# A two-layer sequence kernel: late row tiles planned in two parts, two token tiles normed beside the last rows, and a measured norm in its own tensors

## The chip, the cores and the metric

The kernel runs on one core of a Trainium2 chip. The metric is the device time of the whole program in microseconds (us). It has five kinds of engine queue: TensorE (PE), VectorE (DVE), ScalarE (ACT), GpSimd (POOL) and SyncE (SP), which issues most transfers. Each engine works through its own instructions in order, and engines wait for each other by semaphores only.

## What is computed

`x` is 4 sequences of 1024 tokens with 128 channels, 4096 tokens in all. Four steps follow one another, each on a layer norm of `x` and added to it:

```python
x = x + time_mixing(layernorm(x))   # linear recurrence per head, state = decay * state + k v
x = x + top1_ffn(layernorm(x))      # 8 experts, each token to the one with the largest logit:
                                    #   relu(x W1[e] + b1[e]) W2[e] + b2[e],  D_FF = 512
x = x + memory(layernorm(x))        # quaternion keys and values, cumulative sum along the sequence
                                    #   (this step also adds its own normed input)
x = x + top4_ffn(layernorm(x))      # 32 experts of width 64, 4 per token, and a shared one
```

All is float32. The first two are layer 1 (`mixing_and_top1`), the last two layer 2 (`memory_and_top4`).

## The kernel before

**Tiles.** The tokens are 8 token tiles of 512 (`TILES`, `TILE`), each 4 groups of 128 (`SUB`). `x_tok` stays on chip all the time. A stage of work on tile `i` is written as functions of a step number, 0 to 15; one engine's program is these functions called in a fixed order, each emitting this engine's part.

**Mixing.** `pipeline` (L345) runs, for each `i` and step, `scan(i)`, `tail(i-1)`, `send`, `pick(i-3)`, `ahead(i+1)`, `norm(i+2)`, `measure(i+3)` and `look(i-2)`. The layer norm of tiles 0 to 2 is made by `norm` on VectorE (statistics, steps 2 and 3) and GpSimd (L1331 to L1338, step 4: `var_eps`, `rstd`, `minus_mean`, `shift`). That of tiles 3 to 7 (`i >= MEASURED`) is made by `measure`: ScalarE sums and squares at step 1 (L1115 to L1122), takes the root at step 6 (L1128), and VectorE makes `rstd` and `shift` at steps 8 and 9 (L754, L757). Both use the same three tensors `minus_mean`, `rstd` and `shift`, so ScalarE's `measure(3)` waits for GpSimd's `shift` of tile 2 (`shift_ready, i`). ScalarE's `norm` (L1135) makes `xn` of them. `ahead` turns, mixes and projects: the `tanh` `m1` on ScalarE (L1149, L1157), mixes on TensorE (L481, L484), `lerp` on VectorE (L780), `xf` on GpSimd (L1350).

**Rows.** `pick` finds each token's expert and its place among that expert's rows; GpSimd scatters the normed rows by an indirect transfer into `rows_in` (one region per expert, L1376), each row with the number of the place in `results` that its outcome goes to (`token`). 39 row tiles of 128 rows (`ROW_TILES`) are then worked through: 12 (`EARLY_ROWS`) planned by `early_plan` when five token tiles are counted, and 27 planned by `late_plan` (L991) from the final counts. A plan is, per row tile, its expert and its first row. `late_plan` runs on VectorE inside `closing`, between `pick(7)` and `bias_out(3)`: about fourteen small operations, each behind the one before it by `all_put`, the larger on a grid of 27 row tiles by 8 experts.

For row tile `k` the engines do: SP fetches the rows (L403, three tiles ahead, when `result_row` of tile `k-1` is copied); TensorE transposes (L628), expands (L635, 8 matmul passes) and contracts (L644, 8 passes); ScalarE copies the expert's weights (L1242), the transposed rows (L1247) and makes `relu` (L1252); VectorE adds the first bias (`bias_hidden`, L973), copies the row numbers (L978) and adds the second bias (`bias_out`, L985); GpSimd sends the result rows by an indirect transfer into `results` (`give_back`, L1390). `late_rows` (L366) loops over the first 16 of the 27 (row tiles 12 to 27) and writes the last 11 (28 to 38) out one by one. Per row TensorE's order is `expand(k)`, transpose of `k+1`, `contract(k-1)`. VectorE has two `bias_part`s behind rows 28 and 29.

**Into layer 2.** SP waits until every row tile is stored, then fetches `results` for three token tiles (`bring_back`, L1739). `weave` (L1690) runs `norm(0)`, ten steps of `norm(1)`, `ahead(0)` with the rest of `norm(1)`, and then `body(i)` for each tile: per step `tail(i-1)`, `main(i)`, `ahead(i+1)`, `norm(i+2)`. In layer 2, `norm` is: step 3 VectorE adds the fetched results to `x_tok` (L1957), 4 statistics (L1962), 5 aggregates (L1969), 6 GpSimd makes `shift` (L2308 to L2315), 9 ScalarE makes `xn` (L2186), 12 TensorE transposes (L1797) and ScalarE copies (L2193). `ahead` is: 0 key projection (L1801, L1803), 1 ScalarE copies and squares, 2 VectorE reduces (L1976), 3, 5 and 7 ScalarE's key parts (L2207) and a root, 5 and 6 VectorE's maximum and reciprocal, 4 TensorE's value projection, 7 VectorE scales the values. `main` step 0 makes `bound`. VectorE meets `norm(2,3)` in `body(0)` at step 3.

The lines that the steps above name, beside the functions printed below:

```python
act.wait_ge(decay_ready, n + 1)                      # measure, ScalarE, step 1
act.wait_ge(shift_ready, i)
...
for i in range(BACK_RING):                           # SP, before weave
    bring_back(i)
```

Of the kernel before, what the change touches and what calls it, by code (L numbers as in the profile page):

```python
# [18 lines left out]
P = 128  # L19
BATCH, SEQ = 4, 1024  # L20
TOKENS = BATCH * SEQ
SUB = 4
# [33 lines left out]
def shape_constants():  # L56
# [8 lines left out]
    for k in range(P):  # L65
        for a in range(2):
# [25 lines left out]
LOOPED_ROWS = 16  # L92

B_PARTS = [("strict", P), ("ones", P), ("rank", EXPERTS), ("region", EXPERTS), ("first_row", EXPERTS),
           ("tile_no", ROW_TILES), ("tile_end", ROW_TILES), ("tile_start", ROW_TILES), ("token", GROUPS), ("empty", EMPTY_TILES),
# [4 lines left out]
def shape_constants_b():  # L100
# [13 lines left out]
    part["token"][:] = np.arange(TOKENS).reshape(P, GROUPS)  # L114
    part["empty"][:] = TOKENS + np.arange(EMPTY_TILES * P).reshape(P, EMPTY_TILES)
# [26 lines left out]
def mixing_and_top1(nc, block, x_tok, consts, state_space, rs_space, x_in, w_in, c_in, early, late, top1, b_in, w1_in, w2_in, b1_in, b2_in,  # L142
# [5 lines left out]
    with ExitStack() as ctx:  # L148
# [9 lines left out]
        weights = sb("weights", [P, A_WIDTH])  # L158
        spread = sb("spread", [P, HK * P], F32R)
# [6 lines left out]
        deviation = sb("deviation", [P, SUB])  # L166
        eps_gn = sb("eps_gn", [P, 1])
# [16 lines left out]
        xn = sb("xn", [P, SUB, P])  # L184
        xt = [sb(f"xt{h}", [P, TILE + 1]) for h in range(2)]
        dx = sb("dx", [P, TILE])
        mix1_dx = sb("mix1_dx", [P, P + E_MIX])
        heads_u = sb("heads_u", [P, P])
# [5 lines left out]
        decay = sb("decay", [P, 2, TILE])  # L194
        kk = sb("k", [P, 2, TILE])
        rr = sb("r", [P, 2, TILE])
        vv = sb("v", [P, TILE])
        v_hi = sb("v_hi", [P, 2, TILE], F32R)
        v_lo = sb("v_lo", [P, 2, TILE], F32R)
        table_call = sb("table_call", [P, 1])  # L200
        gate = sb("gate", [P, 2, TILE])
        rku = sb("rku", [P, TILE])
        bonus_v = sb("bonus_v", [P, 2, TILE])
        state = state_space[:, 0:HK * (SEQ + 1)].rearrange("p (j t) -> p j t", j=HK)
        rs = rs_space[:, 0:HK * TILE].rearrange("p (j t) -> p j t", j=HK)
        y_sum = sb("y_sum", [P, TILE])
        yc = sb("yc", [P, TILE])
        yc2 = sb("yc2", [P, TILE])
# [3 lines left out]
        z = sb("z", [P, TILE])  # L212
# [7 lines left out]
        b_ones = sb("b_ones", [P, EXPERTS])  # L220
# [17 lines left out]
        count = sb("count", [P, EXPERTS])  # L238
# [5 lines left out]
        top = sb("top", [P, EXPERTS + 1])  # L244
        climb = sb("climb", [P, EXPERTS])
        ended = sb("ended", [P, ROW_TILES, EXPERTS])
        climbed = sb("climbed", [P, ROW_TILES, EXPERTS])
# [18 lines left out]
        early_count = front[0][:, 4 * SUB * EXPERTS:(4 * SUB + 1) * EXPERTS]  # L266

# [46 lines left out]
        sums_ready, scaled_ready, square_ready, deviation_ready = (sem(name) for name in ("sums", "scaled_mean", "squares", "deviation"))  # L314
        stats_ready, moments_ready, var_ready = sem("stats_ready"), sem("moments_ready"), sem("var_ready")
# [25 lines left out]
        taken_over = [sums_ready, scaled_ready, square_ready, deviation_ready, scaled, spread_ready, mean_ready, stats_ready, moments_ready, var_ready, rstd_ready, shift_ready, xn_ready,  # L341
# [24 lines left out]
        def late_rows(engine, row, beside=None):  # L366
# [5 lines left out]
            for k in range(EARLY_ROWS + STORES * bodies, ROW_TILES):  # L372
                row(k, k % STORES, k // STORES)
                if beside:
                    beside(k - EARLY_ROWS - 8 * bodies)
# [7 lines left out]
        def _(sp):  # L383
# [51 lines left out]
            late_rows(sp, row)  # L435

        @block.tensor
        def _(pe):
# [115 lines left out]
            def pick(i, h, step):  # L554
# [19 lines left out]
                if step == 12:  # L574
# [4 lines left out]
                    if i == 0:  # L579
                        pe.wait_ge(route_set, 1)  # L580
                    if i == EARLY_TOKENS - 1:
# [145 lines left out]
            contract(ROW_TILES - 1, (ROW_TILES - 1) % 2)  # L727

        @block.vector
        def _(dve):  # L730
# [1780 lines left out]
```

## Time and profile before

| what | value |
|---|---|
| median of 3 runs | 820.4 us (819.52 to 821.27) |
| the profiled execution's own time | 819.28 us |
| its span, first to last instruction | 817.3 us |
| TensorE busy | 727.6 us, 89% |
| VectorE / ScalarE / GpSimd busy | 602.2 / 485.6 / 490.0 us |
| mean granted TensorE clock | 0.962 of full |

Times in the rows are microseconds from the start of the span. Busy shares are averages over stages with different limits; what counts for a stage is which wait in it ends last. In a timeline row, the brackets give how long the engine stood idle before the instruction and what released it; "issue" is time in which the profile shows nothing that it waited for. A granted clock of 0.50 is 1.2 GHz, 1.00 is 2.4 GHz. By time: mixing lasts to about 235, `closing` to about 285, the late rows to 342, the memory step to about 480, the top-4 step to the end.

### The profile page before, as it was taken

To read this page: it belongs to the slowest core of one execution; us is meant where nothing else is said; L and a number is where in the kernel's file an instruction comes from. 1 tells how busy PE (TensorE), PEld (TensorE's weight loads), DVE (VectorE), ACT (ScalarE), POOL (GpSimd) and SP (SyncE) were. 2 spreads that over 40 slices of the span, in tenths; PEclk is the share of its full clock that TensorE was granted. 3 is DMA by queue.
4 is the path that set the end of the run, shared out by engine and by line. 5 is a ranking of instruction groups with operands and counts; after the bars stand their busy time and mean duration, and the time that the engine had idled before them with its cause. 6 is when DMAs were issued, how large, how long until landed. Compare 5 with 4: busy or idle time off the path is not lost.

```text
span 817.3 us, 14378 instructions
## 1 busy us (share of the span) xinstructions
PE 727.6 (89%) x4027; PEld 549.6 (67%) x4028; DVE 602.2 (74%) x1377; ACT 485.6 (59%) x1045; POOL 490.0 (60%) x498
## 2 busy tenths in 40 slices
PE   4599999999868799668999979999999999999996
PEld 2345554555447689657888867777778787878784
DVE  3489999999965445347888758786868686868673
ACT  3567778664435367446566556666666665666553
POOL 3577668788753544436878745555555555555564
PEclk9889999999979999859999998999999999999999
DMA  8700000000011355210000036363636364646450
GB/s 246 244 0 1 0 1 14 8 8 14 14 40 44 107 137 142 67 41 28 14 1 1 2 74 137 74 149 79 145 83 140 84 140 89 134 93 132 100 122 13
DMA packets 38265, 60.47 MB, mean 74 GB/s; under 512 B 3776, under 2 KB 17728, under 8 KB 37808
## 3 DMA queue, kind: packets, MB, share of 16 engines
q1 hardware_dynamic: 35920, 54.93, 28.5%
q0 software_dynamic: 2272, 4.67, 1.7%
q8 instruction: 32, 0.52, 0.3%
q14 instruction: 41, 0.34, 0.1%
HBM read 51.31 MB, written 8.28 MB: 73 GB/s over the span
## 4 chain that ended last, share of the span: by engine, by line
PE 66%; DVE 17%; issue 7%; ACT 4%; POOL 2%; DMA 2%; DVEq 1%; another core or an unknown queue 0%; ACTq 0%; POOLq 0%; SPq 0%
DVE state_and_wide L803 4%; PE a_vb L635 4%; PE c_m L1861 4%; PE c_m L1826 4%; PE c_m L1863 3%; PE c_m L1862 3%; PE c_r L1842 3%; PE a_front L481 3%; PE a_vb L644 2%; PE a_y L644 2%; DVE a_vb L787 2%; PE c_v L1861 2%; PE c_r L1911 2%; PE c_r L1910 2%; PE c_r L1913 2%
## 5 line engine op out<-in xcount | busy, mean ns | idle before, releaser
L2379 POOL TENSOR_TENSOR d_hid_lo<-c_bound,d_hid_hi 128x512 fp32r<-128x512 f32 x136 | 175.6, 1292 | 141.3 <-ACT d_hid_hi L2289 139.9
L2289 ACT ACTIVATE d_hid_hi<-c_bound 128x512 fp32r<-128x512 f32 x136 | 85.1, 626 | 38.0 <-DVE c_bound L2160 36.8
L1367 POOL TENSOR_TENSOR ducts_and_memory_weights<-a_r,state_and_wide 128x512 f32<-128x512 f32 x64 | 75.0, 1181 | 25.2 <-DVE state_and_wide L803 19.8
L803 DVE TENSOR_TENSOR_SCAN state_and_wide<-a_decay,state_and_wide,a_vb 128x512 f32<-128x512 f32 x64 | 81.0, 1268 | 0.1
L2151 DVE TENSOR_TENSOR c_m<-c_bound,c_m 128x512 f32<-128x512 f32 x64 | 44.3, 691 | 23.5 <-PE c_m L1863 17.5
L2151 DVE TENSOR_TENSOR c_v<-c_bound,c_v 128x512 f32<-128x512 f32 x64 | 44.3, 692 | 22.0 <-PE c_v L1863 16.3
L1861 PE MATMUL c_m<-d_x_hi,d_hi 128*128 128x512 f32 x136 | 56.3, 414 | 3.6 <-DVE c_bound L2160 3.3
L2279 ACT ACTIVATE c_bound<-c_m 128x512 f32<-128x512 f32 x60 | 35.7, 595 | 33.7 <-PE c_m L1863 33.1
L2279 ACT ACTIVATE c_bound<-c_k 128x512 f32<-128x512 f32 x60 | 35.7, 595 | 33.4 <-PE c_k L1863 32.9
L1863 PE MATMUL c_m<-d_x_hi,d_lo 128*128 128x512 f32 x136 | 54.4, 400 | 0.0
L1862 PE MATMUL c_m<-d_x_lo,d_hi 128*128 128x512 f32 x136 | 54.0, 397 | 0.0
L787 DVE TENSOR_TENSOR a_vb<-a_k,a_vb 128x512 f32<-128x512 f32 x64 | 43.3, 688 | 8.1 <-PE a_vb L535 7.9
L973 DVE TENSOR_TENSOR a_lerp<-a_vb,b_b 128x512 f32<-128x512 f32 x39 | 27.0, 691 | 28.2 <-PE a_vb L635 20.0
L1350 POOL TENSOR_TENSOR a_xf<-a_lerp,a_xt 128x512 f32<-128x512 f32 x32 | 34.7, 1093 | 18.2 <-DVE a_lerp L780 18.1
L635 PE MATMUL a_vb<-a_td_hidden,a_m 128*128 128x128 f32 x312 | 42.5, 281 | 3.4 <-DVE a_lerp L973 1.8
L1376 POOL DMA_INDIRECT rows_in<-a_rows,a_index x32 | 31.9, 996 | 21.3 <-DVE a_index L953 15.2
L2160 DVE TENSOR_TENSOR c_bound<-c_v,state_and_wide 128x512 f32<-128x512 f32 x56 | 38.7, 691 | 7.0 <-DMA state_and_wide<-pair_weights 4.0
L481 PE MATMUL a_front<-a_m,a_weights 128*128 128x512 f32 x64 | 35.2, 644 | 8.5 <-ACT a_m L1149 8.4
L635 PEld LDWEIGHTS a_vb<-a_td_hidden,a_m 128*128 128x128 f32 x312 | 38.9, 197 | 4.4 <-issue 2.9
L2160 DVE TENSOR_TENSOR c_bound<-c_m,state_and_wide 128x512 f32<-128x512 f32 x56 | 38.7, 691 | 2.5 <-POOL d_hid_lo L2379 0.7
L534 PE MATMUL a_vb<-a_v_hi,a_spread 128*128 128x512 f32 x64 | 38.7, 605 | 0.6 <-issue 0.5
L1252 ACT ACTIVATE a_xf<-a_lerp 128x512 f32<-128x512 f32 x39 | 24.5, 629 | 22.8 <-DVE a_lerp L973 8.3
(376 smaller groups left out, 2151.1 us busy)
## 6 DMA issues: line engine op xcount, KB each, us to landing
state_and_wide<-pair_weights SPq DMA_DIRECT2D x64, 512.0 KB, 11.5
b_w<-in_w SPq DMA_DIRECT2D x2, 2048.0 KB, 12.1
state_and_wide<-in_moe SPq DMA_DIRECT2D x16, 204.0 KB
a_xf<-rows_in SPq DMA_DIRECT2D x39, 64.5 KB
state_and_wide<-results SPq DMA_DIRECT2D x8, 256.0 KB, 2.7
out<-c_read SPq DMA_DIRECT2D x8, 256.0 KB, 2.3
a_weights<-in_mixing SPq DMA_DIRECT2D x1, 1077.0 KB, 7.1
shape_consts<-in_consts SPq DMA_DIRECT2D x1, 744.0 KB, 4.4
```

The lines of the kernel that those rows point to most:

```text
L481: mm = pe.matmul(front[n % 3][:, :], w("mix2")[:, f * P:(f + 1) * P], m1[:, 0, :], start=True, stop=True)
L635: mm = pe.matmul(bank_h[h][:, f * P:(f + 1) * P], w1_now[:, h, f * P:(f + 1) * P], xin_t[:, h, :], start=True, stop=True)
L803: dve.tensor_tensor_scan(state[:, j, seq_cols(h, 1)], decay[:, h, :], vb[j % 3][:, :], first, ALU.mult, ALU.add).then_inc(scan_ready, 1)
L1367: pool.tensor_tensor(rs[:, j, :], rr[:, h, :], state[:, j, seq_cols(h, 0)], ALU.mult).then_inc(rs_ready, 1)
L1861: pe.matmul(out, weights_hi, moving_hi, start=start, stop=False)
L1862: pe.matmul(out, weights_hi, moving_lo, start=False, stop=False)
L1863: return pe.matmul(out, weights_lo, moving_hi, start=False, stop=stop)
L2151: dve.tensor_tensor(bank_3[r][:, :], silu[:, r, :], bank_3[r][:, :], ALU.mult).then_inc(product_ready, 1)
L2160: dve.tensor_tensor(hidden[:, r, :], bank_3[r][:, :], w_wide[:, u - 1, :], ALU.mult).then_inc(hidden_ready, 1)
L2279: act.activation(silu[:, r, :], bank_1[r][:, :], ACT.Silu).then_inc(silu_ready, 1)
L2289: act.activation(hid_hi[:, n % HALVES, :], hidden[:, r, :], ACT.Copy).then_inc(hi_ready, 1)
L2379: pool.tensor_tensor(hid_lo[:, n % HALVES, :], hidden[:, r, :], hid_hi[:, n % HALVES, :].bitcast(F32), ALU.subtract).then_inc(lo_ready, 1)
```

## The change

Three things are changed.

1. `measure` writes `minus_measured`, `rstd_measured` and `shift_measured` instead of the tensors that `norm` uses, with semaphores of their own (`inverse_ready`, `measured`). ScalarE's wait at step 1 is now for the previous measured tile, none for the first.
2. The late plan has two parts per expert, 16 parts in all (`PARTS`). The first part of an expert has as many whole row tiles as hold its rows of the first two token tiles (counted by a further matmul, `first_count`, in `pick(2)`); first parts come first. So the results of token tiles 0 and 1 (`FIRST_TOKENS`) are complete when 28 row tiles (`FIRST_ROWS`) are stored. `results` is laid out tile by tile, tiles 0 and 1 at its end; rows that a later row tile repeats go to a place aside (a minimum on VectorE in place of the copy of row numbers, in the last 11 row tiles).
3. The last 11 row tiles are emitted by `memory_and_top4` with a function `beside` called after each. SP fetches the results of tiles 0 and 1 behind row 30 and that of tile 2 when all rows are stored. The norms of tiles 0 and 1 and most of `ahead(0)` stand behind rows 30 to 38 by the table `BESIDE`; the value projection and the transposes of tile 1 follow the last row. Tensors that layer 2 lays its own over are allocated first (`mixing_operands`), and two PSUM banks change places. `weave` begins with `body(0)`.

The diff, cut to its core:

```diff
+FIRST_TOKENS = 2
+FIRST_ROWS = EARLY_ROWS + LOOPED_ROWS
+PARTS = 2 * EXPERTS
+def result_of(i):
+    return TILE * (i - FIRST_TOKENS) if i >= FIRST_TOKENS else OTHERS + ASIDE + TILE * i
...
+        def remaining(name, row, end):
+            def emit(beside):
+                for k in range(EARLY_ROWS + LOOPED_ROWS, ROW_TILES):
+                    row(k, k % STORES, k // STORES)
+                    beside(k - EARLY_ROWS - LOOPED_ROWS)
+                if end:
+                    end()
+            last_rows[name] = emit
...
 measure, VectorE
                 if step == 8:
                     dve.wait_ge(deviation_ready, i - MEASURED + 1)
-                    dve.wait_ge(xn_ready, i)
-                    dve.reciprocal(rstd[:, :], deviation[:, :]).then_inc(rstd_ready, 1)
+                    if i > MEASURED:
+                        dve.wait_ge(xn_ready, i)
+                    dve.reciprocal(rstd_measured[:, :], deviation[:, :]).then_inc(inverse_ready, 1)
...
 measure, ScalarE
                 if step == 1:
                     act.wait_ge(decay_ready, n + 1)
-                    act.wait_ge(shift_ready, i)
+                    need(act, measured, n)
...
 early_plan, VectorE
+                    put(dve.tensor_tensor(first_tiles[:, :], first_tiles[:, :], done[:, :], ALU.subtract))
+                    put(dve.tensor_scalar(part_tiles[:, 0:EXPERTS], first_tiles[:, :], 0.0, None, ALU.max))
+                    all_put()
+                    put(dve.tensor_tensor(first_upto[:, :], part_tiles[:, 0:EXPERTS], done[:, :], ALU.add))
+                    all_put()
+                    put(dve.scalar_tensor_tensor(first_upto[:, :], first_upto[:, :], float(P), route_const("first_row"), ALU.mult, ALU.add))
...
 late_plan, VectorE
-                grid = [P, LATE_ROWS, EXPERTS]
+                grid = [P, LATE_ROWS, PARTS]
...
+                put(dve.tensor_tensor(left[:, :], last_row, first_upto[:, :], ALU.subtract))
+                all_put()
+                put(dve.tensor_scalar(left[:, :], left[:, :], 0.0, float(P - 1), ALU.max, ALU.add))
+                put(dve.tensor_tensor(part_rows[:, first], last_row, first_upto[:, :], ALU.min))
+                put(dve.tensor_copy(part_rows[:, rest], last_row))
...
 layer 2
+        BESIDE = ((), (), ((0, 3), (0, 4)), ((0, 5), (0, 6), (1, 3), (1, 4)), ((0, 9), (1, 5)), ((0, 12), (1, 6)),
+                  (0, 1), (2, 3), (5,), (6, 7), ((1, 9),))      # a pair is norm(tile, step), a number ahead(0, step)
+        def start(norm, ahead, row):
+            for each in BESIDE[row]:
+                if isinstance(each, tuple):
+                    norm(each[0], each[0] % 2, each[1])
+                else:
+                    ahead(0, 0, each)
...
 weave
-            for step in range(STEPS):
-                norm(0, 0, step)
-            for step in range(NORMED_AT):
-                norm(1, 1, step)
-            for step in range(STEPS):
-                ahead(0, 0, step)
-                if step >= NORMED_AT:
-                    norm(1, 1, step)
...
 SP
-            for i in range(BACK_RING):
-                bring_back(i)
+            def beside(row):
+                if row == 2:
+                    sp.wait_ge(loaded["taken"], 1)
+                    stored_rows(FIRST_ROWS)
+                    for i in range(FIRST_TOKENS):
+                        bring_back(i)
+            last_rows["sp"](beside)
+            stored_rows(ROW_TILES)
+            bring_back(FIRST_TOKENS)
...
 TensorE, behind the rows
+            last_rows["pe"](beside)
+            ahead(0, 0, 4)
+            norm(1, 1, 12)
```

## Rows read from the trace of the kernel before

**Rows 1.** Busy time, share of the span and instructions (page, part 1).

```profile
PE 727.6 (89%) x4027; PEld 549.6 (67%) x4028; DVE 602.2 (74%) x1377; ACT 485.6 (59%) x1045; POOL 490.0 (60%) x498
```

**Rows 2.** Waits: who waited for whom: total, times, longest us.

```profile
ACT a_rate L1115 <- POOL a_shift L1338: 8.1, 1, 8.1
```

**Rows 3.** Windows: stretch, length, busy time per engine, PEclk, DMA share, GB/s.

```profile
316.00:324.00 8.00, 8.00 (x73) 7.92 (x72) 5.31 (x20) 6.03 (x13) 4.05 (x5) 1.00 0.47 126
```

**Rows 4.** Timeline of the last rows: start, us, engine, line, what, idle before.

```profile
321.17 0.96 POOL L1390 DMA_INDIRECT results<-a_xf,a_result_row  x1 [0.94 <-issue]
...
322.31 0.55 DVE L1102 TENSOR_TENSOR bias<-ducts_and_memory_weights,bias 1x384 fp32r<-1x384 f32 x1
322.89 0.69 DVE L973 TENSOR_TENSOR a_lerp<-a_vb,b_b 128x512 f32<-128x512 f32 x1
...
323.88 0.29 DVE L985 TENSOR_TENSOR a_dx<-a_y,b_b 128x128 f32<-128x128 f32 x1 [0.24 <-PE a_y L644]
324.78 0.69 DVE L973 TENSOR_TENSOR a_lerp<-a_vb,b_b 128x512 f32<-128x512 f32 x1 [0.60 <-PE a_vb L635]
...
329.30 0.63 ACT L1252 ACTIVATE a_xf<-a_lerp 128x512 f32<-128x512 f32 x1 [0.45 <-issue]
...
339.56 1.15 PE L644 MATMUL a_vb<-b_w,a_xf 128*128 x8 [0.74 <-DVE a_dx L985]
...
341.94 0.96 POOL L1390 DMA_INDIRECT results<-a_dx,a_result_row  x1 [0.93 <-DVE a_dx L985]
```

**Rows 5.** Timeline from the last row into layer 2.

```profile
344.32 1.30 SPq L1739 DMA_DIRECT2D state_and_wide<-results  x3
...
347.43 0.69 DVE L1957 TENSOR_TENSOR x_tok<-x_tok,state_and_wide 128x512 f32<-128x512 f32 x1 [6.28 <-DMA state_and_wide<-results]
348.16 0.87 DVE L1962 BATCH_NORM_STATS2 c_stats<-x_tok 128x6 f32<-128x128 f32 x4
...
350.26 1.05 POOL L2311 TENSOR_TENSOR c_rstd<-c_var_eps,ducts_and_memory_weights 128x4 f32<-128x4 f32 x1
...
351.96 1.65 ACT L2186 ACTIVATE c_xn<-x_tok,c_shift,c_rstd 128x128 f32<-128x128 f32 x4 [12.54 <-POOL c_shift L2315]
...
353.75 1.09 PE L1797 MATMUL c_x<-ident,c_xn 128*128 128x128 f32 x4 [13.04 <-ACT c_xn L2186]
...
360.41 1.22 ACT L2207 ACTIVATE c_key<-c_k 128x256 f32<-128x256 f32 x4
...
367.13 0.68 DVE L1957 TENSOR_TENSOR x_tok<-x_tok,state_and_wide 128x512 f32<-128x512 f32 x1
...
377.82 1.16 PE L1803 MATMUL c_k<-ducts_and_memory_weights,c_xt 128*128 128x128 f32 x8
```

**Rows 6.** Timeline of the first mixing stage, 36 to 52 us.

```profile
36.64 0.31 ACT L1115 ACTIVATE a_rate<-x_tok 128x128 f32<-128x128 f32 x1 [8.09 <-POOL a_shift L1338]
...
39.74 0.57 ACT L1149 ACTIVATE a_m<-a_front 128x512 f32<-128x512 f32 x1
...
42.48 0.75 DVE L780 SCALAR_TENSOR_TENSOR a_lerp<-a_front,a_weights,a_dx 128x512 f32<-128x512 f32 x1 [6.85 <-PE a_front L481]
...
43.31 1.09 POOL L1350 TENSOR_TENSOR a_xf<-a_lerp,a_xt 128x512 f32<-128x512 f32 x1 [5.72 <-DVE a_lerp L780]
...
50.85 1.09 POOL L1350 TENSOR_TENSOR a_xf<-a_lerp,a_xt 128x512 f32<-128x512 f32 x1 [0.42 <-DVE a_lerp L780]
```

**Rows 7.** Timeline of VectorE, late plan and what follows it.

```profile
266.28 0.38 DVE L1005 TENSOR_TENSOR a_ended<-a_end_tile,b_consts 128x216 f32<-128x216 f32 x1
...
268.57 0.28 DVE L985 TENSOR_TENSOR a_xf<-a_y,b_b 128x128 f32<-128x128 f32 x1
```

**Rows 8.** Windows of TensorE: stretch, length, busy time, PEclk, DMA share, GB/s.

```profile
274.00:276.00 2.00, 0.24 (x2) 1.00 0.14 33
...
343.00:344.00 1.00, 0.00 (x0) 0.50 0.20 66
```

**Rows 9.** Chain that ended last: start, us, what.

```profile
245.02 2.73 PE a_vb L635 x16
```

More of the change, by code:

```diff
@@ L364, in pick_step, with late_rows @@
             return step + 4 if i == EARLY_TOKENS - 1 else step
-        def late_rows(engine, row, beside=None):
+        def late_rows(engine, row):
             bodies = LOOPED_ROWS // 8
@@ L371, in late_rows @@
                     row(STORES * b + EARLY_ROWS + n, (EARLY_ROWS + n) % STORES, b + (EARLY_ROWS + n) // STORES)
[L372 to L375, printed above, removed]
+        last_rows = {}
+        def remaining(name, row, end):
[6 more added lines that the diff above has]
+            last_rows[name] = emit
         MEASURED = 3
@@ L580, in pick @@
                         pe.wait_ge(route_set, 1)
+                    if i == FIRST_TOKENS:
+                        pe.matmul(first_count, ones_b[:, :], total[:, h, :], start=True, stop=True)
                     if i == EARLY_TOKENS - 1:
@@ L1131, in norm @@
                 if step == (8 if i < MEASURED else 1):
-                    act.wait_ge(shift_ready, i + 1)
+                    if i < MEASURED:
+                        act.wait_ge(shift_ready, i + 1)
+                        by, less = rstd, shift
+                    else:
+                        act.wait_ge(measured, i - MEASURED + 1)
+                        by, less = rstd_measured, shift_measured
                     need(act, xt_ready, i)
@@ L1135, in norm @@
                         a = act.activation(xn[:, s, :], x_tok[:, SUB * i + s, :], ACT.Identity,
-                                           bias=shift[:, s:s + 1], scale=rstd[:, s:s + 1])
+                                           bias=less[:, s:s + 1], scale=by[:, s:s + 1])
                     a.then_inc(xn_ready, 1)
@@ L1431, in _ @@
             late_rows(pool, row)
-            give_back(ROW_TILES - 1, (ROW_TILES - 1) % STORES)
+            remaining("pool", row, lambda: give_back(ROW_TILES - 1, (ROW_TILES - 1) % STORES))
         for each in taken_over:
             nc.release_semaphore(each)
+        return last_rows
 QUATS, QC = P // 4, 4
@@ L1946, in end, with beside @@
                     mm.then_inc(yt_out, 1)
-            pe.wait_ge(bias_ready, 1)
-            pe.wait_ge(loaded["taken"], 1)
+            def beside(row):
+                if row == 5:
+                    pe.wait_ge(bias_ready, 1)
+                    pe.wait_ge(loaded["taken"], 1)
+                start(norm, ahead, row)
+            last_rows["pe"](beside)
+            ahead(0, 0, 4)
+            norm(1, 1, 12)
             weave(pe, norm, ahead, main, tail, look, route, unit, end)
@@ L2174, in end, with beside @@
                                       bank_z[:, :].rearrange("p (s c) -> p s c", s=SUB), ALU.add).then_inc(out_ready, 1)
-            dve.wait_ge(loaded["taken"], 1)
+            def beside(row):
+                if row == 2:
+                    dve.wait_ge(loaded["taken"], 1)
+                for each in BESIDE[row]:
+                    if isinstance(each, tuple):
+                        norm(each[0], each[0] % 2, each[1])
+                    elif each < 7:
+                        ahead(0, 0, each)
+            last_rows["dve"](beside)
+            ahead(0, 0, 7)
             weave(dve, norm, ahead, main, tail, look, route, unit, end)
@@ L2297, in end, with beside @@
                     act.activation(y_sb[:, :], bank_y[h][:, :], ACT.Copy).then_inc(y_ready, 1)
+            def beside(row):
+                if row == 2:
+                    act.wait_ge(loaded["taken"], 1)
+                start(norm, ahead, row)
+            last_rows["act"](beside)
+            norm(1, 1, 12)
             act.wait_ge(moe_loaded, 16 * PIECES)
-            act.wait_ge(loaded["taken"], 1)
             weave(act, norm, ahead, main, tail, look, route, unit, end)
@@ L2383, in end, with beside @@
                 pass
-            pool.wait_ge(bias_ready, 1)
-            pool.wait_ge(loaded["taken"], 1)
+            def beside(row):
+                if row == 3:
+                    pool.wait_ge(bias_ready, 1)
+                    pool.wait_ge(loaded["taken"], 1)
+                start(norm, ahead, row)
+            last_rows["pool"](beside)
             weave(pool, norm, ahead, main, tail, look, route, unit, end)
```

201 lines of the change are left out of this document (133 added, 68 removed).

## The prediction

> **What bounds the kernel now.** I read the busy shares first: TensorE is busy 89% of the span, VectorE 74% [rows 1], so a change pays only where TensorE stands idle. The table of waits then names such places, and two belong to this change. One is early: ScalarE waits 8.1 us at L1115 for GpSimd's `shift`, and `m1`, for which TensorE waits, stands behind it on ScalarE [rows 2]. The other is between the layers. In the late rows TensorE has no gap (8.00 of 8 us at full clock from 316 to 324 [rows 3]), and they go by at one per 1.9 us (bias additions at 322.89 and 324.78 [rows 4]). But the last row tile's contraction starts at 339.56, its result is sent at 341.94, the fetch of the results goes out at 344.32, the addition that needs it starts at 347.43, and TensorE waits 13.04 us until the transposes of tile 0 [rows 5]; they start right behind the four `xn` of 351.96.
>
> **Part 1, the measured norm in own tensors.** Before, `measure(3)` writes `minus_mean`, so ScalarE must wait until GpSimd has made `shift` of tile 2. Its idle time of 8.09 us ends at 36.64, so it was free at 28.55; its eight passes and what belongs to them last until `m1` at 39.74, 3.1 us [rows 6]. With own tensors the wait goes: `m1` starts at 28.55 + 0.05 + 3.1 = 31.7, 8.0 us earlier. What is late next? VectorE: it waits 6.85 us for the mix (42.48), so it is free at 35.63 [rows 6]. By then the first mix is there (`m1` 31.7, its tanh 0.57, a matmul of under 2 us even at half clock). The first `lerp` moves 42.48 - 35.63 = 6.85 us forward, and later ones by up to ScalarE's 8.1. GpSimd is the tighter one: `shift` of tile 2, which frees ScalarE at 36.6, and one state product of the size of an `xf`, 1.1 us, keep it until about 37.6, while before it began its first `xf` at 43.31: 5.7 us forward. From there to the end of the fifth (50.85 + 1.09 = 51.94) took 8.6 us though five `xf` and one product of 1.09 to 1.27 are 6.7; with VectorE ahead of it they go back to back: about 44.4, 7.5 us forward [rows 6]. Behind it stand `v_lo` and the next stage's spreading, so I take **7.5 us**; the ends are 5.7 (only the first `xf`'s gain lasts) and 8.1 (the whole wait). ScalarE still meets the wait for tile 2's `shift` in `norm(2)`, at 36.5, but the `tanh` behind it isn't due before 40.
>
> **Part 2, the plan in two parts.** `late_plan` gets 16 columns for 8. Its 27 x 8 comparison takes 0.38 us [rows 7]; at twice the elements each of the four such passes costs about 0.22 us more (the row less some 0.15 us for a pass with few elements), 0.9 us, and one more dependent step 0.2 us. It ends right where the waiting `bias_out(3)` starts (268.57 [rows 7]), and TensorE waits for that: +1.1 us. The three operations in `pick(2)` and four in `early_plan`, some 0.2 us each with their waits, stand on a VectorE that is nearly full there: 1.4 us at most, half counted. Sum **+1.8 us**, ends 0 and 3. The extra count matmul and the `min` for the cast cost nothing that shows. A contiguous fetch instead of a strided one I cost at nothing: each partition still reads 2 KB.
>
> **Part 3, two tiles normed beside the last 11 rows.** First what it can give. The order on VectorE has `norm(2,3)` in `body(0)`, which needs tile 2's results and so every row. It ran at 367.13; the same addition for tile 0 started 3.1 us behind the fetch [rows 5]. If the rows ended as before, it could now run at 344.32 + 3.1 = 347.4, so the transition gains 19.7 us less S, where S is by how much the inserted work delays the last row.
>
> Now S. A row leaves VectorE 0.6 us between a `bias_out` and the next bias addition (323.88 + 0.29 to 324.78), and an inserted bias rounding of 0.55 us fitted into such a gap (322.31) [rows 4]. ScalarE has about 0.4 us a row (0.45 before 329.30 [rows 4]), TensorE nothing. All queues are in order. I carried each engine's order through rows 30 to 38 with these durations:
> - Row 30. Row 27's results are sent at 321.17; by the last row (341.94 to 344.32) they are stored 2.4 us later, so the fetch goes out at 323.6 and lands at 326.6. VectorE has been free since 324.17: it stands 2.5 us, then 0.68 for the addition and 0.87 for the statistics. Row 31's bias addition stands behind this wait, and `relu`, contraction and GpSimd's return behind that. Less the gap of 0.6 and slips: 3.2 us.
> - Rows 31 and 32. GpSimd begins the norm only behind `give_back(30)` (0.8 until it starts, 0.96); then 0.2, 1.05 (the power, 350.26), 0.2 and 0.2 with their waits. VectorE's statistics of tile 1 wait for the first of these, ScalarE for the last, and then ScalarE has 1.65 us of `xn` [rows 5] ahead of row 32's `relu`: 4.3 us.
> - Row 33: transposes 0.45 on TensorE, copy 0.6 on ScalarE behind them, and `relu` behind that: 2.1 with what is left of the row before. Row 34: the key projection takes TensorE 1.5 (its eight passes 1.16 [rows 5]; the bias pass and a gap 0.4), then ScalarE two copies of 0.5 to 0.6: with the slack of the late row 0.9 beyond. Row 35: 0.6 of key parts (four took 1.22) and the root, which waits for VectorE's reduction (0.69, as for any 128x512): 1.3. Rows 36 to 38: two more pairs of key parts, a reciprocal of under 1, `xn` 1.65, partly in slack: 1.2.
>
> S = 3.2 + 4.3 + 2.1 + 0.9 + 1.3 + 1.2 = **13.0 us**. No row of before shows such a mix, so the ends: S can't be below the 1.9 us added to TensorE, which has no gap; were nothing hidden and five rows at half clock, S = 8.2 (VectorE) + 7.4 (ScalarE) + 2 (GpSimd) + 2.9 + 6 (TensorE) = 26.5. The transition then gains 19.7 - 13.0 = 6.7 by the fetch. VectorE's own way there is slightly longer: contraction issued to 340.45 + 13.0 = 353.45, then value projection 1.5, values 1.1, first `bound` 0.64, sums 0.9, next key projection 1.5, square 1.1, reduction 0.7, each with a hand-over of 0.05 to 0.3: 361.1 against 367.13. I take **6.0 us**.
>
> **The clock, and a rule against the change.** In the trace TensorE's granted clock stayed at full through a stretch in which it worked 0.24 of 2 us (274 to 276), and was at half in the third microsecond after the last contraction [rows 8]. The new waits of rows 31 and 32, some 3 to 4 us each, lie between the two. The Trainium skill, "TensorE: Matmul & The Clock Gate", section "HAM oscillation — how this bites in real kernels", says that a loop whose matmuls wait for transfers each time falls back to the slow clock and pays its return each time. Counted by rows: eight row matmuls take 0.9 us at full (two times eight and a transpose in the pitch of 1.9) and 1.4 at half clock (245.02: 16 in 2.73 [rows 9]), so five rows with both at half clock cost up to 5 us on TensorE, of which 2 to 3 come through behind the other waits.
>
> **The sum.** -7.5 + 1.8 - 6.0 = -11.7 us. The profiled execution took 819.28 (span 817.3 and 2.0 around it), so 807.6; the median of the runs is 1.1 above it: **808.7 us**.
>
> **The rivals.**
> - The rows hide the norms better (S about 6, as VectorE's waits overlap ScalarE's): 808.7 - 7 = 801.7. For it: the bias rounding that cost nothing. Against: the wait for the fetch on VectorE has nothing beside it.
> - The transition gives nothing (S about 19, the clock at half through five rows and the row loads late behind 512 KB of fetches): 808.7 + 6 = 814.7. For it the gaps named above.
> - Part 1's gain is given back in stage 1, since GpSimd has the products of stage 0 still to do: 3 of 7.5 left, 813.
> - Slower than before: the eleven last rows become a chain of four engines. VectorE waits for the fetch, GpSimd for VectorE behind its own sends, ScalarE for GpSimd, TensorE for ScalarE, in every row with work beside. It decides once S passes 19.7 + 7.5 - 1.8 = 25.4; at the upper end of 26.5, 821.5, and a little beyond with body(0) at half clock, 823. Against it: only rows 30 to 32 hold a fetch or GpSimd's chain.
>
> **How the numbers follow.** Forecast 0.55 (own range 804.5 to 813), better hidden 0.14, nothing from the transition 0.15, given back 0.05, slower 0.07; 0.04 for sums that cancel. A difference of 0.2% is about what a measurement can tell from none. Faster 0.88, same 0.04, slower 0.08. The range leaves out the best tenth of the hidden case and the slow ones: 801 to 817.
>
> **What would show it.** ScalarE's wait at L1115 gone from the start, `m1` at about 31.7, `closing` some 6 us earlier, a late plan of 4.8 us for 3.7. In the last rows: VectorE waiting 2 to 3 us for `come_back` behind row 30, the contraction of row 31 over 3 us late, 11 rows in some 34 us rather than 21, and `norm(2,3)` near 355 instead of 367.13. The forecast is wrong if the row pitch stays near 2 us (then 800), or if clock and pitch fall for all 11 rows.

## The result and the profile after

| | before | after |
|---|---|---|
| median of 4 runs each | 820.12 us (819.52 to 821.27) | 808.56 us (806.41 to 809.93) |
| profiled execution, its span | 819.28, 817.3 us | 809.93, 808.1 us |
| mean granted clock | 0.962 | 0.972 |

The ratio is 0.9852, with a 95% interval of 0.9828 to 0.9877. 808.7 us was predicted. The profiled execution was the slowest of the four after, so the two traces differ by only 9.2 us of span. All ratios are of fast executions; a single slow one, of 1839.72 us in e11, stays out.

I compare the traces by *lead*: how much earlier an instruction starts in a changed kernel's trace than the same one in the trace before. The lead is 7.5 us from stage 1 on (first spreading of `v` at 48.05 for 55.55), 6.7 behind `pick(2)`, 5.7 at 247, 3.3 at row 28's bias addition (315.88 for 319.19), -9.8 at the last contraction, 10.2 at `norm(2,3)`, 11.0 through the memory step and 9.2 at the end.

Mixing, timeline of ScalarE, GpSimd and TensorE after. ScalarE's wait of [rows 2] is gone, `m1` starts at 31.87 for 39.74, the five `xf` end at 44.4, and the wait for tile 2's `shift` is met at `xn` instead:

```profile
31.87 0.57 ACT L1253 ACTIVATE a_m<-a_front 128x512 f32<-128x512 f32 x1
36.92 1.65 ACT L1239 ACTIVATE a_xn<-x_tok,a_shift,a_rstd 128x128 f32<-128x128 f32 x4 [2.68 <-POOL a_shift L1442]
42.26 2.15 POOL L1454 TENSOR_TENSOR a_xf<-a_lerp,a_xt 128x512 f32<-128x512 f32 x2
48.05 0.47 PE L599 MATMUL a_vb<-a_v_hi,a_spread 128*128 128x512 f32 x1 [0.72 <-issue]
```

The late plan, timelines of VectorE. Before, from its first operation to `bias_out(3)` (268.57 [rows 7]), 3.6 us:

```profile
264.98 0.15 DVE L997 TENSOR_TENSOR a_count<-a_tail,b_consts 128x8 f32<-128x8 f32 x1
```

After, its first operation, the first of the four wide passes and `bias_out(3)`, 5.1 us from first to last:

```profile
260.04 0.15 DVE L1083 TENSOR_TENSOR a_left<-a_tail,a_first_upto 128x8 f32<-128x8 f32 x1
261.59 0.61 DVE L1097 TENSOR_TENSOR a_decay<-a_part_end,b_consts 128x432 f32<-128x432 f32 x1
265.11 0.28 DVE L1071 TENSOR_TENSOR a_xf<-a_y,b_b 128x128 f32<-128x128 f32 x1
```

The last rows, timelines after, which answer to [rows 4, 5]. VectorE waits for the fetch, GpSimd for VectorE, ScalarE for GpSimd's `shift`, and TensorE for ScalarE; the last contraction is at 349.37 for 339.56, the third tile's addition at 356.91 for 367.13:

```profile
323.39 0.69 DVE L2081 TENSOR_TENSOR x_tok<-x_tok,state_and_wide 128x512 f32<-128x512 f32 x1 [2.52 <-DMA state_and_wide<-results]
325.66 0.63 ACT L1356 ACTIVATE a_xf<-a_lerp 128x512 f32<-128x512 f32 x1 [3.84 <-DVE a_lerp L1055]
326.43 2.07 PE L711 MATMUL a_y<-b_w,a_xf 128*128 x8 [3.11 <-ACT a_xf L1356]
326.82 0.96 POOL L1495 DMA_INDIRECT results<-a_dx,a_result_row  x1 [4.21 <-DVE c_moments L2093]
329.71 1.65 ACT L2320 ACTIVATE c_xn<-x_tok,c_shift,c_rstd 128x128 f32<-128x128 f32 x4 [2.34 <-POOL c_shift L2455]
332.02 1.41 PE L711 MATMUL a_vb<-b_w,a_xf 128*128 x8 [2.04 <-ACT a_xf L1356]
338.70 0.60 ACT L2335 ACTIVATE c_key<-c_k 128x512 f32<-128x512 f32 x1 [2.19 <-PE c_k L1920]
349.37 1.15 PE L711 MATMUL a_vb<-b_w,a_xf 128*128 x8 [0.90 <-ACT a_xf L1356]
356.91 0.69 DVE L2081 TENSOR_TENSOR x_tok<-x_tok,state_and_wide 128x512 f32<-128x512 f32 x1 [0.26 <-DMA state_and_wide<-results]
```

Windows after (the column behind the five engines' busy times is the granted clock). The first three lie in the rows, the fourth where TensorE meets the top-4 step:

```profile
326.00:328.00 2.00, 1.57 (x7) 1.57 (x8) 0.89 (x6) 1.09 (x3) 1.15 (x2) 0.50 0.13 37
328.00:330.00 2.00, 1.97 (x12) 1.73 (x10) 1.44 (x5) 0.29 (x1) 1.46 (x4) 0.66 0.11 37
334.00:336.00 2.00, 2.00 (x12) 2.00 (x11) 0.00 (x0) 1.63 (x3) 1.24 (x3) 0.50 0.07 20
486.00:488.00 2.00, 2.00 (x6) 1.53 (x5) 0.28 (x4) 0.83 (x2) 0.20 (x1) 0.50 1.06 222
```

Over the whole span the clock was at half for 62 us before and 45 after; TensorE was busy in 37 of these before, 33 after.

### The profile page after: what moved, and what is told of

Its sections match the earlier page's. It is cut to its first block, busy times and chain, and to the rows that moved or that the text cites. A ratio compares the mean times of both kernels' runs of the same rounds, so it can differ in the third digit from the quotient of the medians.

```text
span 808.1 us, 14393 instructions
## 1 busy us (share of the span) xinstructions
PE 728.6 (90%) x4028; PEld 550.1 (68%) x4029; DVE 605.7 (75%) x1387; ACT 484.4 (60%) x1045; POOL 490.4 (61%) x498
## 4 chain that ended last, share of the span: by engine, by line
PE 44%; DVE 6%; issue 1%; ACT 1%; DMA 1%; POOLq 0%; DVEq 0%; SPq 0%; POOL 0%; ACTq 0%
PE c_m L1978 3%; PE c_r L1959 3%; PE c_m L1980 3%; PE c_m L1979 3%; PE c_m L1943 3%; PE c_v L1978 2%; PE c_v L1980 2%; PE c_k L1978 2%; PE c_r L2028 2%; PE c_v L1979 2%; PE c_r L2027 2%; PE c_r L2030 2%; PE c_k L1979 2%; PE c_k L1980 2%; PE c_o L2030 2%; PE c_o L2028 2%
## 5 line engine op out<-in xcount | busy, mean ns | idle before, releaser
L702 PE MATMUL a_vb<-a_td_hidden,a_m 128*128 128x128 f32 x312 | 44.4, 289 | 3.4 <-DVE a_lerp L1055 2.1
L702 PEld LDWEIGHTS a_vb<-a_td_hidden,a_m 128*128 128x128 f32 x312 | 40.9, 205 | 4.4 <-issue 2.9
L1454 POOL TENSOR_TENSOR a_xf<-a_lerp,a_xt 128x512 f32<-128x512 f32 x32 | 34.7, 1095 | 10.5 <-DVE a_lerp L848 10.4
L1495 POOL DMA_INDIRECT results<-a_xf,a_result_row x20 | 19.2, 961 | 28.7 <-DVE a_xf L1071 15.5
## 6 DMA issues: line engine op xcount, KB each, us to landing
state_and_wide<-pair_weights SPq DMA_DIRECT2D x64, 512.0 KB, 11.5
```

Source lines behind the costliest of these rows:

```text
L702: mm = pe.matmul(bank_h[h][:, f * P:(f + 1) * P], w1_now[:, h, f * P:(f + 1) * P], xin_t[:, h, :], start=True, stop=True)
```

## The experiments

Each ran five times or more, in turns with the kernel before on the same chip. Ratios are to that one; in us they are times 820.

**e1 and e2: parts alone.** e1 is the kernel before with the measured tensors only:

```diff
-                    dve.wait_ge(xn_ready, i)
-                    dve.reciprocal(rstd[:, :], deviation[:, :]).then_inc(rstd_ready, 1)
+                    if i > MEASURED:
+                        dve.wait_ge(xn_ready, i)
+                    dve.reciprocal(rstd_measured[:, :], deviation[:, :]).then_inc(inverse_ready, 1)
 (and shift_measured, minus_measured likewise)
```

> The kernel before with nothing but the measured norm in tensors of its own. Theory (the wait at the first measure is worth 7.5 us and the gain lasts to the end, since every later stage is bound by its own engines): 7.5 us faster than before, about 812.5. Rival (part of the lead is swallowed by the closing and the rows, where it fell from 7.5 to 3.3 us in the changed kernel, and not by the planning): 3 to 4 us faster, about 816.5.

Measured: 814.55 us (before 821.13), ratio 0.9917 (0.9893 to 0.9941): -6.8 us, with an interval (4.8 to 8.8) that holds the theory's 7.5 and not the rival's 3 to 4. Its lead is 7.4 up to 226, then falls to 4.1 in the late rows although no plan is changed, and is 5.7 in the memory step. Windows of the stretch where it falls, before and in e1. TensorE's half clock lies otherwise, and TensorE has more of its work in it:

```profile
216.00:228.00 12.00, 5.37 (x28) 3.16 (x26) 11.69 (x31) 5.98 (x12) 8.07 (x8) 0.79 0.06 18
228.00:240.00 12.00, 9.34 (x57) 5.54 (x58) 8.48 (x31) 4.86 (x12) 5.49 (x6) 0.78 0.10 29
```

```profile
216.00:228.00 12.00, 6.25 (x28) 2.90 (x28) 10.44 (x29) 2.85 (x7) 7.42 (x7) 0.57 0.07 23
228.00:240.00 12.00, 10.79 (x57) 9.16 (x54) 4.99 (x20) 4.72 (x13) 3.83 (x4) 0.64 0.15 45
```

From 213 to 276, TensorE was busy 13.8 us at half clock before, 19.3 in e1 (218 to 228, 231 to 242, 269 to 272) and 17.1 after. At half clock a row's eight matmuls took 2.07 us for 1.15, about twice as long, so as an estimate this is 2.8 us of e1's loss of 3.3, and 1.7 of the 4.2 after.

But the traces of the later runs say that the lead is not what brings it. e7, e11 and e12 have the same lead (7.4, 6.8 and 7.2 us) and 13.5, 14.1 and 13.5 us of such work, and e8, which has no lead, has 17.1. What differs is mostly a third stretch of 3.4 us at half clock between 250 and 300, which the trace before and these three lack. Up to row 28 nine traces run the same code as the changed kernel on chips on which the kernel before takes 820 to 821 us. Between stage 1 and row 28 they lose, in us: e12 -0.6, e7 0.6, e11 1.2 (the three without the third stretch), e2 1.4, e6 1.8, e4 2.3, e3 2.8, e5 3.8 and after 4.2. So a loss of this size there varies from one execution to the next, and one trace can't put it down to an edit.

e2 is the changed kernel with all norms behind the last row again:

```diff
-            last_rows["pe"](beside)
-            ahead(0, 0, 4)
-            norm(1, 1, 12)
+            last_rows["pe"](lambda row: None)
 (the other engines likewise; SP fetches three tiles at the end)
+            for step in range(STEPS):
+                norm(0, 0, step)
 (and norm(1), ahead(0), as the kernel before has them)
```

> The changed kernel with the plan in two parts and the measured tensors, but all fetches, norms and ahead(0) behind the last row as before. Theory: it keeps the lead of 3.3 us that the changed kernel has at row 28, so 3 to 4 us faster than before, and the changed kernel is some 6 to 8 us faster than this one, which is what the work beside the rows is worth. Rival (the lead at row 28 is lost to the placement of tensors and code, and the transition gives less than 5 us net): below 1 us from the changed kernel's time less 5.

Measured: 814.02 us (before 821.13), ratio 0.9928 (0.9903 to 0.9954): -5.9 us. Against e1 on the same chip it is 0.5 us faster by the medians and 0.9 slower by the ratios. So the plan's cost can't be told from nothing, and the whole of part 3's gain (after against e2) is some 6 us.

**e8: the plan alone.** e2 with `rstd`, `shift` and `minus_mean` shared again, so the kernel before with the two-part plan.

> The kernel before with the plan in two parts alone: 16 parts, the new layout of the results with its minimum, the count of the first two tiles; no measured tensors, nothing beside the last rows, and the norms behind the last row as before. Theory of the prediction: 1.8 us slower than the kernel before (ends 0 and 3), 822.9 us where that one shows 821.1. Rival (the 4.2 us that the changed kernel lost between stage 1 and the late rows are all the plan's): 825.3. Second rival (the plan lies beside TensorE's own work and costs nothing, as the kernel with plan and measured tensors is no slower than that with measured tensors alone): 820.6.

Measured: 818.86 us (before 820.23), ratio 0.9991 (0.9971 to 1.001): between -2.4 and +0.8 us. The sum's 1.8 and the 4.2 of the rival are both outside, and the second rival (no cost) came out. The added time on VectorE is there, yet the lead at row 28 is only 0.7 us lower than in stage 1, and `pick(2)` alone had taken 0.8. What takes up the late plan's rest is VectorE's own next wait, before and in e8:

```profile
268.57 0.28 DVE L985 TENSOR_TENSOR a_xf<-a_y,b_b 128x128 f32<-128x128 f32 x1
271.13 0.29 DVE L985 TENSOR_TENSOR a_dx<-a_vb,b_b 128x128 f32<-128x128 f32 x1 [2.28 <-PE a_y L644]
```

```profile
272.07 0.28 DVE L1066 TENSOR_TENSOR a_xf<-a_y,b_b 128x128 f32<-128x128 f32 x1
272.44 0.29 DVE L1066 TENSOR_TENSOR a_dx<-a_vb,b_b 128x128 f32<-128x128 f32 x1
```

The first of the two is 3.5 us later than before, the second 1.3: the wait of 2.28 us behind the plan is gone.

**e4: the clock held up for row 31.** The changed kernel with extra matmuls of constants, 12 ahead of row 31's contraction and 6 ahead of row 32's, so that TensorE works through its waits:

```diff
+                if isinstance(k, int):
+                    for _ in range({32: 12, 33: 6}.get(k, 0)):
+                        pe.matmul(tail_bank[:, 0:P], ident, ident, start=True, stop=True)
                 contract(k - 1, 1 - h)
```

> The changed kernel with 12 and 6 further 128x128 matmuls into a bank that is free, on TensorE ahead of the contractions of rows 31 and 32, where it waited 3.1 and 2.0 us. Theory (the fall of the granted clock in these two waits costs little, since the other engines set the pitch there): the clock stays at full from 322 to 340 and the time falls by 1 to 2 us. Rival (clock is the main cost of the delayed rows): 4 us or more faster. A third: the added matmuls end too late and cost up to 1 us.

Measured: 808.64 us (before 821.13), ratio 0.9847 (0.9824 to 0.9871), no gain over the changed kernel, neither the theory's 1 to 2 us nor the rival's 4. Timeline of TensorE and windows of e4: row 31's contraction now runs at full clock (1.15 us for 2.07), but row 32's still runs partly at the lower one (1.65), since the clock falls from 331.0 to 334.4 instead. So the clock did not stay at full as expected; of the rows' work at half clock 3.4 us are left, where it was 6.3 after:

```profile
324.90 1.15 PE L711 MATMUL a_y<-b_w,a_xf 128*128 x8 [0.30 <-ACT a_xf L1359]
330.48 1.65 PE L711 MATMUL a_vb<-b_w,a_xf 128*128 x8 [1.98 <-ACT a_xf L1359]
```

```profile
326.00:328.00 2.00, 2.00 (x19) 2.00 (x19) 0.98 (x5) 0.00 (x0) 1.76 (x5) 1.00 0.23 67
332.00:334.00 2.00, 2.00 (x11) 2.00 (x10) 0.29 (x1) 0.98 (x2) 0.65 (x1) 0.50 0.15 33
```

And yet the bias additions of rows 32 to 38 have lost 5.9, 5.9, 8.9, 10.5, 11.5, 12.8 and 13.0 us against row 28, where it is 6.1, 6.1, 8.9, 10.7, 11.7, 13.0 and 13.1 after. The work that went back to full clock was not what these rows waited for.

**e5, e6, e3, e7: the table of the last rows.** Only `BESIDE` and what follows the last row change. A pair is norm(tile, step), a number a step of `ahead(0)`:

```diff
 e5, all one row later
+BESIDE = ((), (), (), ((0, 3), (0, 4)), ((0, 5), (0, 6), (1, 3), (1, 4)), ((0, 9), (1, 5)), ((0, 12), (1, 6)),
+          (0, 1), (2, 3), (5,), (6,))                        # behind: 7, (1, 9), 4, (1, 12)
 e6, the fetch as it was, the rest further apart
+BESIDE = ((), (), ((0, 3), (0, 4)), ((0, 5), (0, 6)), ((1, 3),), ((0, 9), (1, 4)), ((0, 12), (1, 5), (1, 6)),
+          (0, 1), (2,), (3,), ())                            # behind: (1, 9), 5, 6, 4, 7, (1, 12)
 e3, both
+BESIDE = ((), (), (), ((0, 3), (0, 4)), ((0, 5), (0, 6)), ((1, 3),), ((0, 9), (1, 4)), ((0, 12), (1, 5), (1, 6)),
+          (0, 1), (2,), (3,))                                # behind: (1, 9), 5, 6, 4, 7, (1, 12)
 e7, later still
+BESIDE = ((), (), (), (), ((0, 3),), ((0, 4), (0, 5), (0, 6)), (), ((0, 9), (1, 3)), ((0, 12), 0, (1, 4), (1, 5), (1, 6)),
+          (1, 2), (3,))                                      # behind: 5, 4, 6, (1, 9), 7, (1, 12)
```

> The changed kernel with another table: the first addition behind row 31 rather than row 30 (the fetch has landed by then), each further step a row or two later, so that no engine waits for another one beside a row; the key parts, the root's followers, xn of tile 1 and its transposes behind the last row, where 7 us pass anyway until tile 2's results are there. Theory (13 us of delay come from waits of engines in order, about half of them avoidable): the rows are delayed by 6.8 us instead of 13.1, the norm of tile 2 starts 6 us earlier, about 802.5. Rival (the delay is the work itself, and what is moved behind the last row comes back there): within 1.5 us of the changed kernel.

> The changed kernel with its table moved by one row tile as a whole: the addition of the fetched tile 0 stands behind row 31, not 30, and what was beside each row is beside the next; the last pieces follow the last row. Only the wait for the fetch should go. Theory (each wait of the prediction's row list is a term of its own, and the delay S of the last row is their sum): VectorE's stand of 2.5 us for the fetch behind row 30 is gone, the wait behind the chain GpSimd - ScalarE stays and moves to row 33; S falls by about 3 and the time with it, 808.6 - 3 = 805.6 us. Rival (the chain sets the pace, the fetch was hidden beside it, so that taking it away alone gives nothing): 808 to 809. Second rival (the clock: any row with a gap of 2 us or more costs more than the gap): 803.5 if TensorE's clock then stays at full in the rows.

> The changed kernel with the addition of tile 0 behind row 30 as it was, so with the wait for the fetch, but with the pieces that depend on one another across engines (statistics, GpSimd's shift, ScalarE's xn, the transposes, the projection) set one or two row tiles further apart, as in the kernel with everything spread. Theory (terms of their own): the waits of rows 31 to 36 shrink by some 4.4 us, the fetch's wait stays; 808.6 - 4.3 = 804.3 us, and with the kernel that is one row later the two gains add up to that of the spread kernel (803.0) within 2 us. Rival (the fetch's wait is what drops the clock and puts every queue behind): over 807.

> The spread kernel with its pieces later again: nothing beside rows 28 to 31, tile 0's addition behind row 32, its statistics behind 33, xn and tile 1's addition behind 35, transposes, key projection and tile 1's statistics behind 36, the rest behind the last row. Carrying the queues through with the durations of the trace gives a last row 1.5 us earlier than in the spread kernel and the third tile's norm 1.5 us earlier as well: 803.0 - 1.5 = 801.5 us. Rival (what is taken from the rows comes back behind the last row, where the chain to the third tile's norm is then the longer one): 803 to 805.

Measured: e3 802.99 us (before 821.13), ratio 0.9789 (0.9766 to 0.9812), -17.3 us. e5 803.86 (before 820.23), 0.9803 (0.9780 to 0.9826), -16.2. e6 801.53, 0.9782 (0.9758 to 0.9805), -17.9. e7 799.24, 0.9755 (0.9731 to 0.9780), -20.1. e3 came within 0.5 us; e5, e6 and e7 missed by 1.7, 2.8 and 2.3 us, all on the good side. Their last rows don't explain that: S came out larger than carried through in each, as the table below shows.

First additions of tile 0, VectorE's timeline, in e6, e3 and e7. The wait for the fetch stays in e6 (2.53), nearly goes in e3 and is gone in e7:

```profile
321.50 0.69 DVE L2088 TENSOR_TENSOR x_tok<-x_tok,state_and_wide 128x512 f32<-128x512 f32 x1 [2.53 <-DMA state_and_wide<-results]
```

```profile
322.66 0.69 DVE L2088 TENSOR_TENSOR x_tok<-x_tok,state_and_wide 128x512 f32<-128x512 f32 x1 [0.40 <-DMA state_and_wide<-results]
```

```profile
321.08 0.68 DVE L2088 TENSOR_TENSOR x_tok<-x_tok,state_and_wide 128x512 f32<-128x512 f32 x1
```

Timelines of e5, and a window of it. The fetch's wait is nearly gone, but ScalarE's for GpSimd is now 3.11 us where it was 2.34, and TensorE's 3.60. The granted clock is 1.00 all the while, so the chain alone stops the rows, without the clock:

```profile
323.65 0.69 DVE L2088 TENSOR_TENSOR x_tok<-x_tok,state_and_wide 128x512 f32<-128x512 f32 x1 [0.67 <-DMA state_and_wide<-results]
330.48 1.65 ACT L2323 ACTIVATE c_xn<-x_tok,c_shift,c_rstd 128x128 f32<-128x128 f32 x4 [3.11 <-POOL c_shift L2458]
332.78 1.15 PE L711 MATMUL a_y<-b_w,a_xf 128*128 x8 [3.60 <-ACT a_xf L1356]
```

```profile
328.00:334.00 6.00, 2.40 (x22) 2.16 (x21) 2.97 (x13) 2.84 (x7) 3.23 (x6) 1.00 0.14 38
```

For every kernel, S is the lead at row 28's bias addition less that at the last contraction, and the gain is the lead at `norm(2,3)` less that at row 28:

| kernel | S carried through beforehand | S | gain | S + gain |
|---|---|---|---|---|
| after | 13.0 | 13.1 | 6.9 | 20.0 |
| e4 | | 13.0 | 6.7 | 19.7 |
| e5 | 10.1 | 10.6 | 9.5 | 20.0 |
| e6 | 8.7 | 9.2 | 10.8 | 20.0 |
| e3 | 6.8 | 7.6 | 12.6 | 20.2 |
| e7 | 5.3 | 6.9 | 13.1 | 20.0 |
| e7 again (e11) | 5.3 | 6.9 | 13.3 | 20.2 |
| e10 again (e12) | 3.4 | 5.7 | 11.0 | 16.7 |
| e10 | 3.4 | 5.8 | 10.3 | 16.1 |
| e9 | about 3 | 4.9 | 9.3 | 14.2 |

The transition gives what the sum said, 19.7 less S, in the first seven lines within 0.5 us. S and gain added are the lead at `norm(2,3)` less that at the last contraction, so a steady 20.0 says one thing: from the last contraction to the third tile's addition it takes 7.4 to 7.9 us in these kernels, where it took 27.6 before. S repeats between two traces of one kernel (6.9 and 6.9, 5.8 and 5.7), the lead at row 28 doesn't (6.8 and 5.6, 9.8 and 7.8).

e5's and e6's medians gain 1.4 and 1.9 us more against the changed kernel than these gains do, which is within the intervals (2 us each); their spans also hold less half clock (35 us each for 45). Two things hold the comparison of S back. e3, e6 and e7 also move four steps behind the last row, and e5 two, so not all of what S falls by comes of the spreading. And in the rows TensorE had 6.3 us of work at half clock after, 3.1 in e6 and none in e5, e3 and e7, so the clock's share is not told apart from the waits'.

**e9 and e10: where it ends.**

```diff
 e9, tile 0 alone
+BESIDE = ((), (), (), (), ((0, 3),), ((0, 4), (0, 5), (0, 6)), (), ((0, 9),), ((0, 12),), (), ())
+          # behind: 0, 1, (1, 3), (1, 4), (1, 5), (1, 6), 2, 3, 5, 4, 6, (1, 9), 7, (1, 12)
 e10, key projection last
+BESIDE = ((), (), (), (), ((0, 3),), ((0, 4), (0, 5), (0, 6)), (), (), ((1, 3), (0, 9), (1, 4), (1, 5), (1, 6)),
+          ((0, 12),), (0,))                                  # behind: 1, 2, 3, 5, 4, 6, 7, (1, 9), (1, 12)
```

> The changed kernel with nothing but the norm of tile 0 and its transposes beside the last rows (addition behind row 32, statistics behind 33, xn behind 35, transposes behind 36); the key projection of tile 0 and the whole norm of tile 1 follow the last row. So far the delay S of the last row and the gain at the third tile's norm added up to 20.0 us in five kernels. Theory: that sum holds only while the third tile's fetch ends last; here S falls to some 3 us, but VectorE's own chain behind the last row (norm of tile 1, key projection, reduction, root, reciprocal, values, bound) ends last, and the transition gains 12.4, not 17: sum 15.3, time 800 us or a little above, no better than e7 (799.2). Rival (every microsecond off S is a microsecond off the time): 795.5.

> Between e7 and the kernel with tile 0 alone: statistics of both tiles beside the rows, transposes of tile 0 behind row 37, its key projection behind row 38, and all that ScalarE does with the keys behind the last row. Carrying the queues through gives S = 3.4 us (5.3 in e7) and the third tile's norm 0.1 us earlier than in e7: theory 799 us, the same as e7 within what can be told. Rival (the rows' gain comes through in full): 797; second rival (what is behind the last row costs TensorE's clock): 802.

Measured: e9 800.27 us, ratio 0.9848 (0.9822 to 0.9874); e10 799.15, 0.9829 (0.9800 to 0.9858). Both ran on a chip on which the kernel before takes 812.52, so their times don't stand beside the others'. e9's 800.27 looks like the 800 that was expected, but that was meant for a chip where the kernel before takes 820; by its ratio e9 is only 12.5 us faster than before. Its rival, 795.5, didn't come either way. e7 and e10 were run once more on one chip:

> The kernel of e7 again, beside that of e10 on one chip, since e9 and e10 ran on a chip on which the kernel before takes 812.5 us, not 820.2. The traces say that from the late rows to the third tile's norm e7 gains 13.1 us and e10 10.3, with 0.4 more lost to the clock in e10. Theory: this kernel is 2.8 to 3.2 us faster than e10's. Rival (the equal medians of 799 are the truth): within 1 us of it. On a chip like the first ones, about 799 us; on the other, about 793.

> The kernel of e10 again on the same chip as e11. Theory: 2.8 to 3.2 us slower than e11, so about 802 us where the kernel before takes 820, 796 where it takes 812.5. Rival: within 1 us of e11.

Measured: e11 801.96 us (before 821.3), ratio 0.9757 (0.9731 to 0.9783); e12 803.36, 0.9777 (0.9751 to 0.9802). e10's kernel is 1.4 us slower by the medians, half of what was expected, and the intervals of the two ratios overlap, so no difference is shown. In the traces the sum of S and gain falls to 16 or 17, and 14 for e9, so less delay in the rows brought less at the end. What is behind the last row in e9, timelines and windows: TensorE waits 3.14 us for ScalarE's `xn` of tile 1, its clock falls, and 16 passes take 3.50 us with VectorE behind them:

```profile
342.58 0.74 PE L1921 MATMUL c_x<-ident,c_xn 128*128 128x128 f32 x4 [3.14 <-ACT c_xn L2322]
346.60 3.50 PE L1950 MATMUL c_m<-c_bound,ducts_and_memory_weights 128*128 128x128 f32 x16
348.02 0.69 DVE L2106 TENSOR_REDUCE c_norm<-c_square 128x128 f32<-128x512 f32 x1 [3.55 <-ACT c_square L2339]
```

```profile
338.00:342.00 4.00, 1.44 (x9) 1.00 (x9) 3.13 (x11) 3.60 (x10) 2.22 (x5) 1.00 0.27 69
346.00:350.00 4.00, 4.00 (x21) 4.00 (x21) 1.95 (x6) 2.11 (x6) 0.94 (x1) 0.52 0.00 0
```

The same 16 passes in e7's timeline of TensorE, at full clock:

```profile
344.87 1.95 PE L1951 MATMUL c_m<-c_bound,ducts_and_memory_weights 128*128 128x128 f32 x16
```

## Why the prediction was right

**Part 1 (-7.5): right in size, and all of it reached stage 1.** `m1` was forecast for 31.7 (31.87), the end of the five `xf` for 44.4 (44.41), the gain behind them for 7.5 (7.50). GpSimd did set it: it works without a gap up to the fifth. Alone the part is worth 6.8 us, with 4.8 to 8.8 as the interval. What I had not counted is that the lead between stage 1 and row 28 shrinks by anything from nothing to 4 us from trace to trace.

**Part 2 (+1.8): mis-sized.** The term's parts were found on VectorE: the late plan 1.5 us longer (forecast 1.1), `pick(2)` 0.8 us (forecast 0.7 together with `early_plan`). But they hardly add to the time: e8 bounds the plan at 0.8 us or less. The step that failed is "TensorE waits for that: +1.1 us": the next `bias_out` waited 2.28 us for TensorE anyway. The lead of 4.2 us that went between stage 1 and row 28 looks like the plan's, and isn't: e1 loses 3.3 us there with the old plan. In the profile after, 0.8 us is `pick(2)` and an estimated 1.7 the clock's. Of the other 1.7 no run names the cause, and the same code lost only 0.6 in e7's trace.

**Part 3 (-6.0): the mechanism right, S closer than its terms.** After against e2 is 6.2 us by the ratios. S was 13.1 us for 13.0, step by step on VectorE's bias additions: 3.5 us by row 31 (forecast behind row 30: 3.2), 2.6 by row 33 (4.3), 2.8 by row 34 (2.1), 2.8 by row 36 (2.2), 1.4 from there to the last contraction (1.2). The term of rows 31 and 32, GpSimd's chain and `xn`, was 1.7 us too large and the four others together 1.8 too small, so that the sum hit within 0.1 us is luck. The wait for the fetch was 2.52 us (2.5). The transition gave 6.9 us. That S is a sum of separate waits is borne out only in part: e5, without the fetch's wait, has 2.5 us less and e6, with the chain spread, 3.9 less, together 6.4, and e3 with both has 5.5 less. `norm(2,3)` ended its wait on the fetch, not on VectorE's own way, as I had it, but VectorE had been free for only 0.26 us. My sum for VectorE's way also left just 0.2 us for seven hand-overs that it put at 0.05 to 0.3 each.

**The clock.** The granted clock did fall where forecast: 0.50 and 0.66 from 326 to 330, behind TensorE's wait of 3.11 us. The Trainium skill, "TensorE: Matmul & The Clock Gate", section "HAM oscillation — how this bites in real kernels", has a loop pay for each such return; the fall is as it says here, while in e5 a wait of 3.60 us between the rows brought none. The price I named, 2 to 3 us coming through, is not borne out: e4 took away about half of the rows' work at half clock and every row behind had the same delay, and e5 has an S of 10.6 without any. No run held the clock at full with the table of the changed kernel, so a small price stays open. In the top-4 step 9.4 us of TensorE's work ran at half clock after a wait that ended at 480.4, 6.8 before, and the lead fell from 11.0 to 9.2; of that an estimated 1.3 us is the clock's. This too varies: e7's trace has 2.9 us of such work there and e9's none.

**The rivals.** "Better hidden" (801.7) is what e3, e6 and e7 made of the table, at 803.0, 801.5 and 799.2 with S of 7.6, 9.2 and 6.9; in the kernel as it is VectorE's wait had ScalarE's and GpSimd's behind it. Nothing from the transition, and the slower case, would have needed S of 19 and over 25.

**The total** came out within 0.2 us in part by luck. By the ratios the three parts are -6.8 (e1), +0.9 (e2 against e1) and -6.2 us (after against e2), where -7.5, +1.8 and -6.0 were forecast: the errors of the first two cancel, and each is within its interval of 2 us or more.

## What to carry to other kernels

When work is set into a loop whose engines are in lockstep, count each piece by the queue behind it, not by its own length, and where one engine must wait for another's piece, put the two a round or two apart. The 14 steps that e7 has beside the rows had delayed row 36 by 11.7 us when packed; spread, they delay the last row by 6.9, and the kernel went from 0.985 of the time before to 0.976. Stop where what is left behind the loop becomes the longer chain. And before a lost microsecond is put down to an edit, run the other edits without it and read a second trace of the same code: here nine traces of the same code lost between -0.6 and 4.2 us over one stretch, in part by where the clock was slow.

## What the hardware showed that I had not expected

The kernel before takes 820 to 821 us on three chips and 812.5 on a fourth, at the same mean granted clock (0.963 there, 0.960 on the others). In e9's and e10's traces the lead grows by 4.0 and 4.3 us between 247 and 304, in `closing` and the first late rows, where it grows by 0.3 to 2.0 in e7, e11 and e12; the rest I did not find. The ratio of e10's kernel is 0.983 on that chip and 0.978 on another, with intervals that just touch.
